# Layer norms applied on ScalarE as scale and bias per token, with the bias formed on GpSimd, in an adaLN transformer block

## The chip, the cores and the metric

The kernel runs on one core of a Trainium2 chip. The metric is the device time of one execution in microseconds, the median of several runs; a separate profiled execution gives the trace. Engines are named as in the profile: PE (TensorE), PEld (its weight loads), ACT (ScalarE), DVE (VectorE), POOL (GpSimd), SP (SyncE, which issues the loads and stores).

## What is computed

One transformer block with adaptive layer norm: 8 blocks (batch rows) of 256 tokens, 128 features. Windowed attention with 16 heads of 8 features, and a mixture of 8 experts of 64 hidden features, of which 2 are chosen.

```python
def _layernorm(x, axis=-1, eps=1e-05):
    m = jnp.mean(x, axis=axis, keepdims=True)
    v = jnp.var(x, axis=axis, keepdims=True)
    return (x - m) / jnp.sqrt(v + eps)
...
    x = L0_attn_x
    mod = (_silu(L0_c) @ L0_wmod).reshape(L0_c.shape[0], 6, 1, -1)
    sa, ca, ga, sb, cb, gb = (mod[:, 0], mod[:, 1], mod[:, 2], mod[:, 3], mod[:, 4], mod[:, 5])
    ga = (2 * (ga >= 0) - 1) * jnp.maximum(jnp.abs(ga), 0.25)
    gb = (2 * (gb >= 0) - 1) * jnp.maximum(jnp.abs(gb), 0.25)
    h = _layernorm(x, axis=-1) * (1 + ca) + sa
    x = x + ga * _L0_attn_ref(h, L0_attn_W_qkv, L0_attn_W_o)
    h = _layernorm(x, axis=-1) * (1 + cb) + sb
    x = x + gb * _L0_ffn_ref(h, L0_ffn_gate_weight, ...)
```

## The kernel before

The 8 blocks go through a software pipeline of 8 steps, written out by hand as one `step` function per engine; semaphores join them. Each engine works strictly in the order of its own `step`. Step i holds the attention of block i, the output projection and second norm of block i-1 (the flag `tail`), the expert layer of block i-2 (`ffn`), and the first norm and the query and key projection of block i+1 (`pre`). In step 1 there is no `ffn`; step 7, the last, has no `pre`; what then remains of blocks 6 and 7 stands behind the loop. The 256 tokens of a block are two tiles (NT = 2) of 128 tokens on the partitions.

A layer norm has four parts. VectorE makes mean and variance (`norm_stats`, L784 and L787, into `mv1` or `mv2`). GpSimd adds eps (L306) and raises to the power -1/2 (L309, `rstd`). VectorE subtracts the mean and multiplies by `rstd`, one instruction per tile (L792, `xn1` for the first norm, `xn2` for the second). TensorE transposes the two tiles (L521), and ScalarE applies the modulation while copying out of PSUM (L389 `h_t`; L411 `h2_t`, then L414 `h2_hi`).

The names that the prediction uses:
- `block_max` (L816) and `row_maximum` (L827, then L834, `shift`) are VectorE's part of the softmax; `subtract_max` (L569) is the TensorE instruction that adds `shift` to the scores; L437 is the exponential on ScalarE.
- The scores are L554, ended by the mask L561. `keep_k` (L807, `k_bd`) and `keep_q` provide keys and queries of the next block; the scores of the next step need both.
- `keep_v` (L404, `v_bd`) is 16 small ScalarE copies. `tanh_gate` (L450), VectorE's `activate` (L907 `gate_a`, L911 `act`), GpSimd's `weigh_experts` (L325, `act_w`), the transposes L638, ScalarE's `act_t` (L454) and the down projection L645 are the expert layer. `low_part` (L337, `h2_lo`) is GpSimd's and follows `act_w` in its queue.
- `logits` (L596) gives the router's input; `route_input` (L419, `ex`) and then `route_compare` (from L872, `exp1`) work on it.
- At the start GpSimd splits the expert weights (L369 `w_hi`, L371 `w_lo`), and VectorE's `finish_modulation` (L959 to L970) makes the gates out of the modulation; it stands behind the first `block_max` of step 0.

In the trace the digits of buffers are left out: `xn`, `h_t`, `x` stand for `xn1` and `xn2`, `h_t` and `h2_t`, `x1`.

## Time and profile before

| | us |
|---|---|
| median of 3 runs | 202.34 (202.28 to 204.95) |
| profiled execution, whole | 204.01 |
| its span, first to last instruction | 202.2 |
| busy: PE / PEld / DVE / ACT / POOL | 157.6 / 131.6 / 151.1 / 99.0 / 49.8 |
| granted TensorE clock, mean | 0.932 |

The span is what the trace's times count in; 1.8 us of the execution lie around it. Busy time is a sum over stages with different limits, so it doesn't say by itself which engine sets the time.

### The profile page before, as it was taken

The page shows a single profiled execution, that of the slowest core. Times are in us where ns is not written, and L with a number is a line of the kernel's source. Part 1 is how long each engine was busy: PE and PEld are TensorE (multiplying, and loading weights), DVE is VectorE, ACT ScalarE, POOL GpSimd, SP SyncE. Part 2 cuts the span into 40 slices and gives each one's busy share as a digit, 9 for nine tenths or more (in the row PEclk, how much of TensorE's full clock was granted, in tenths as well). Part 3 has the DMA queues.
Part 4 walks back from the last instruction along what each step waited for, and adds up shares of the span by engine and source line. Part 5 has one row for each costly group of instructions (what it writes and reads, how often), then busy time and mean ns, then how long its engine had stood idle before and what let it go on. Part 6 is the DMA issues. An engine that isn't in the chain of part 4 may idle for free.

```text
span 202.2 us, 5145 instructions
## 1 busy us (share of the span) xinstructions
PE 157.6 (78%) x1948; PEld 131.6 (65%) x1948; DVE 151.1 (75%) x459; ACT 99.0 (49%) x262; POOL 49.8 (25%) x79
## 2 busy tenths in 40 slices
PE   1766987599877978699777978797779977994954
PEld 1556876488756956588466846595569856873734
DVE  2576346739979897958979897989794987877592
ACT  2162363834394538643567338552943366552311
POOL 5080000320053015302143205320530222225121
PEclk9995899856999999969999999999996999999699
DMA  5800000000000010001000010000000000010001
GB/s 175 268 6 3 0 3 2 28 3 0 3 0 3 0 54 3 3 0 49 6 3 5 22 33 0 0 3 26 5 0 3 26 3 2 0 31 0 0 0 52
DMA packets 5832, 4.17 MB, mean 21 GB/s; under 512 B 816, under 2 KB 5296, under 8 KB 5808
## 3 DMA queue, kind: packets, MB, share of 16 engines
q1 hardware_dynamic: 5664, 3.84, 6.5%
q8 instruction: 15, 0.25, 0.5%
q14 instruction: 9, 0.07, 0.1%
q10 hardware_dynamic: 144, 0.00, 0.0%
HBM read 2.80 MB, written 1.05 MB: 19 GB/s over the span
## 4 chain that ended last, share of the span: by engine, by line
DVE 33%; PE 29%; issue 21%; ACT 13%; POOL 1%; DMA 1%; DVEq 0%; ACTq 0%; POOLq 0%
DVE blkmax L816 9%; ACT v_bd L404 8%; PE ps L569 7%; DVE xn L792 6%; PE ps L645 5%; PE ps L585 4%; DVE gate_a L907 3%; DVE shift L834 3%; PE ps L554 2%; ACT probs L437 2%; DVE eall L862 2%; PE ps L693 2%; DVE row_max L827 1%; PE ps L623 1%; PE ps L521 1%
## 5 line engine op out<-in xcount | busy, mean ns | idle before, releaser
L816 DVE TRANSPOSE_TENSOR_REDUCE blkmax<-ps 128x11 f32<-128x352 f32 x64 | 31.1, 524 | 15.3 <-PE ps L561 15.3
L325 POOL TENSOR_TENSOR act_w<-act,cw 128x512 f32<-128x512 f32 x15 | 15.7, 1045 | 70.1 <-issue 49.5
L585 PE MATMUL ps<-probs,v_bd 128*36 128x64 f32 (+2 forms) x640 | 24.7, 235 | 8.5 <-ACT v_bd L404 8.5
L585 PEld LDWEIGHTS ps<-probs,v_bd 128*36 128x36 f32 x640 | 22.7, 119 | 12.8 <-issue 12.4
L437 ACT ACTIVATE probs<-ps 128x704 f32<-128x704 f32 x32 | 23.0, 755 | 15.0 <-PE ps L569 15.0
L404 ACT ACTIVATE v_bd<-ps 32x64 f32<-32x64 f32 x128 | 27.5, 214 | 1.8 <-PE ps L541 0.4
L569 PE MATMUL ps<-shift,quad_ones 128*128 128x384 f32 x64 | 17.8, 408 | 11.0 <-DVE shift L834 11.0
L554 PEld LDWEIGHTS ps<-q_sb,k_bd 32*128 32x128 f32 x640 | 19.9, 192 | 3.3 <-issue 2.6
L554 PE MATMUL ps<-q_sb,k_bd 32*128 32x96 f32 (+2 forms) x640 | 21.9, 279 | 0.0
L569 PEld LDWEIGHTS ps<-shift,quad_ones 128*128 128x128 f32 x64 | 11.6, 215 | 13.9 <-DVE shift L834 13.3
L450 ACT ACTIVATE tanh_g<-ps 128x512 f32<-128x512 f32 x16 | 9.6, 598 | 19.1 <-PE ps L625 19.0
L645 PE MATMUL ps<-wd_sb,act_t 128*128 128x128 f32 x128 | 17.8, 296 | 0.7 <-ACT act_t L454 0.7
L645 PEld LDWEIGHTS ps<-wd_sb,act_t 128*128 128x128 f32 x128 | 17.2, 214 | 1.0 <-ACT act_t L454 0.9
L807 DVE TENSOR_TENSOR k_bd<-ps,con 128x1024 f32<-128x1024 f32 x8 | 9.8, 1225 | 10.1 <-issue 4.6
L638 PE MATMUL ps<-con,act_w 128*128 128x128 f32 x64 | 10.3, 284 | 7.3 <-POOL act_w L325 5.5
L623 PE MATMUL ps<-w_hi,h_hi 128*128 128x512 f32 x32 | 14.6, 457 | 1.6 <-DVE act L911 1.4
L343 POOL TENSOR_TENSOR out_sb<-y_g,x 128x256 f32<-128x256 f32 x7 | 5.1, 727 | 39.3 <-DVE y_g L939 39.3
L444 ACT ACTIVATE o_t<-ps 36x512 f32<-36x512 f32 x16 | 9.5, 592 | 9.7 <-PE ps L585 9.5
L638 PEld LDWEIGHTS ps<-con,act_w 128*128 128x128 f32 x64 | 6.8, 142 | 10.6 <-POOL act_w L325 7.3
L454 ACT ACTIVATE act_t<-ps 128x512 f32<-128x512 f32 x16 | 9.4, 591 | 8.3 <-PE ps L638 8.3
L625 PE MATMUL ps<-w_hi,h_lo 128*128 128x512 f32 x32 | 13.3, 417 | 0.0
L834 DVE TENSOR_TENSOR shift<-row_max,con 128x256 fp32r<-128x256 f32 x32 | 12.7, 439 | 0.6
(98 smaller groups left out, 287.8 us busy)
## 6 DMA issues: line engine op xcount, KB each, us to landing
x_sb<-x SPq DMA_DIRECT2D x8, 128.0 KB, 2.6
out<-out_sb SPq DMA_DIRECT2D x7, 128.0 KB, 1.8
wgu_sb<-w_gu SPq DMA_DIRECT2D x1, 512.0 KB, 3.9
con<-consts SPq DMA_DIRECT2D x1, 284.0 KB, 3.2
wm_sb<-wmod SPq DMA_DIRECT2D x1, 256.0 KB, 4.0
...
```

The lines of the kernel that those rows point to most:

```text
L325: nc.gpsimd.tensor_tensor(act_w[:, t, :].rearrange("p (e i) -> p e i", e=E), act[:, t, :].rearrange("p (e i) -> p e i", e=E), view(cw[:, t ...
L404: last = nc.scalar.activation(dst, src, ACT.Copy)
L437: nc.scalar.activation(probs[:, t, hgs, cols], ps[:, hgs, cols], ACT.Exp, scale=float(DH) ** -0.5).then_inc(probs_ready, 1)
L554: nc.tensor.matmul(view(ps[:, hg, at:at + 1], [[(QBT - 1) * KB, hi - lo + 1], [1, KB]]), k_bd[rows, kb].rearrange("p g k -> p (g k)"), vie ...
L569: last = nc.tensor.matmul(ps[:, hg, 0:CELLS * KB], quad_ones[:], view(shift[:, hg, 0:1], [[0, 3], [1, QBT * KB]]), start=False, stop=True, ...
L585: last = nc.tensor.matmul(ps[p0:p0 + VW, OB, c0 + lo * KB:c0 + (hi + 1) * KB], v_bd[:, kb, hg, :], view(probs[:, t, hg, at:at + 1], [[-(QB ...
L623: nc.tensor.matmul(ps[:, bank, :], h2_hi[:, tok], w_hi[:, w], start=True, stop=False)
L625: last = nc.tensor.matmul(ps[:, bank, :], h2_lo[:, tok], w_hi[:, w], start=False, stop=True)
L638: last = nc.tensor.transpose(ps[:, W0 + t, c * 128:(c + 1) * 128], act_w[:, t, c * 128:(c + 1) * 128], ident)
L645: last = nc.tensor.matmul(ps[:, down_bank(b, t), t * D:(t + 1) * D], act_t[:, t, c, :], wd_sb[:, c, :], start=(c == 0), stop=(c == NC_ - 1))
L816: nc.vector.tensor_reduce(blkmax[:, t, hg, live(t):live(t) + LIVE], view(ps[:, hg, live(t) * KB:live(t) * KB + 1], [[KB, LIVE], [1, KB]]), ...
L834: nc.vector.tensor_tensor(shift[:, pair * PAIR:(pair + 1) * PAIR].rearrange("p h (q k) -> p (h q) k", k=KB), view(row_max[:, pair * PAIR, ...
```

## The change

The normalised value (x - mean) * rstd is written as x * rstd + (-mean * rstd). GpSimd makes the two numbers per token: a negation of the mean beside the eps addition, and, behind the pow, a product (`shift1`, `shift2`; not the `shift` of the softmax). ScalarE applies them with one Identity activation per tile, with scale and bias read from memory; VectorE's two instructions per norm and the two functions that held them go. VectorE's `norm_stats` gets a wait so that `mv` is not overwritten before GpSimd has used it.

```diff
@@ -300,16 +301,19 @@
 
         @block.gpsimd
         def _(pool):
-            def norm_scale(b, var, mv, veps, step_done, rs, used, ready):
+            def norm_scale(b, var, mv, veps, negm, step_done, rs, rs_done, used, sh, ready):
 
                 wait(pool, var, b, NT, NT)
                 nc.gpsimd.tensor_scalar(veps[:], mv[:, :, 1], EPS, None, ALU.add).then_inc(step_done, 1)
-                wait(pool, step_done, b, 1, 1)
+                nc.gpsimd.tensor_scalar(negm[:], mv[:, :, 0], -1.0, None, ALU.mult).then_inc(step_done, 1)
+                wait(pool, step_done, b, 2, 2)
                 wait(pool, used, b, NT, 0)
-                nc.gpsimd.tensor_tensor(rs[:], veps[:], minus_half[:], ALU.pow).then_inc(ready, 1)
+                nc.gpsimd.tensor_tensor(rs[:], veps[:], minus_half[:], ALU.pow).then_inc(rs_done, 1)
+                wait(pool, rs_done, b, 1, 1)
+                nc.gpsimd.tensor_tensor(sh[:], negm[:], rs[:], ALU.mult).then_inc(ready, 1)
 
             def scale_x(b):
-                norm_scale(b, ln1_var, mv1, veps1, eps1_step, rstd1, xn1_ready, rstd1_ready)
+                norm_scale(b, ln1_var, mv1, veps1, negm1, eps1_step, rstd1, rstd1_step, xn1_ready, shift1, shift1_ready)
 
             def scale_wo(i):
 
@@ -328,7 +332,7 @@
                     view(cw[:, t, :], [[1, E], [0, I]]), ALU.mult).then_inc(actw_ready, 1)
 
             def scale_x1(i):
-                norm_scale(i, ln2_var, mv2, veps2, eps2_step, rstd2, xn2_ready, rstd2_ready)
+                norm_scale(i, ln2_var, mv2, veps2, negm2, eps2_step, rstd2, rstd2_step, xn2_ready, shift2, shift2_ready)
 
             def low_part(i):
 
@@ -382,6 +386,21 @@
 
         @block.scalar
         def _(act_e):
+            def normalise(b, xs, rs, sh, sh_ready, xn, ready):
+
+                wait(act_e, sh_ready, b, 1, 1)
+                for t in range(NT):
+                    nc.scalar.activation(xn[:, t, :], xs[:, t, :], ACT.Identity, scale=rs[:, t:t + 1],
+                                         bias=sh[:, t:t + 1]).then_inc(ready, 1)
+
+            def norm1_apply(b):
+                wait(act_e, xt_ps, b, 1, 0)
+                normalise(b, x_sb[:, b % XBUF], rstd1, shift1, shift1_ready, xn1, xn1_ready)
+
+            def apply_norm2(i):
+                wait(act_e, h2t_ps, i, 1, 0)
+                normalise(i, x1[:, i % 2], rstd2, shift2, shift2_ready, xn2, xn2_ready)
+
             def modulate_x(b):
 
                 wait(act_e, xt_ps, b, 1, 1)
@@ -469,10 +488,14 @@
                     keep_gates(2 * i + 1)
                 if i > 0:
                     keep_v(i)
+                if tail:
+                    apply_norm2(i - 1)
                 if ffn:
                     tanh_gate(i - 2, 1)
                 if tail:
                     modulate_h2(i - 1)
+                if pre and i > 0:
+                    norm1_apply(i + 1)
                 if i < 2:
                     modulate_x(i + 1)
                 if ffn:
@@ -492,11 +515,13 @@
             nc.scalar.preload_act_table(ACT.Exp)
             act_e.wait_ge(c_loaded, 16)
             nc.scalar.activation(ct_t[:], ct_sb[:], ACT.Tanh, scale=0.5).then_inc(tanh_c_ready, 1)
+            norm1_apply(0)
             act_e.wait_ge(mod1_ready, 2)
             modulate_x(0)
             act_e.wait_ge(zeroed, 3)
             keep_q(0)
             keep_v(0)
+            norm1_apply(1)
             steps(step)
 
             keep_o(B - 1)
@@ -504,6 +529,7 @@
             keep_on(B - 1)
             tanh_gate(B - 2, 1)
             keep_act_t(B - 2, 0)
+            apply_norm2(B - 1)
             modulate_h2(B - 1)
             route_input(B - 1)
             keep_act_t(B - 2, 1)
@@ -778,27 +804,18 @@
 
         @block.vector
         def _(dve):
-            def norm_stats(b, xs, stats, stat, mv, var):
+            def norm_stats(b, xs, stats, stat, mv, var, used):
 
                 for t in range(NT):
                     nc.vector.bn_stats(stats[:, t, :], xs[:, t, :]).then_inc(stat, 1)
                 wait(dve, stat, b, NT, NT)
+                wait(dve, used, b, 1, 0)
                 for t in range(NT):
                     nc.vector.bn_aggr(mv[:, t, :], stats[:, t, :]).then_inc(var, 1)
 
-            def normalise(b, xs, mv, rs, rs_ready, xn, ready):
-                wait(dve, rs_ready, b, 1, 1)
-                for t in range(NT):
-                    nc.vector.tensor_scalar(xn[:, t, :], xs[:, t, :], mv[:, t, 0:1], rs[:, t:t + 1],
-                                            ALU.subtract, ALU.mult).then_inc(ready, 1)
-
             def norm1(b):
                 wait(dve, x_loaded[b % XBUF], b // XBUF, 16, 16)
-                norm_stats(b, x_sb[:, b % XBUF], stats1, ln1_stat, mv1, ln1_var)
-
-            def norm1_apply(b):
-                wait(dve, xt_ps, b, 1, 0)
-                normalise(b, x_sb[:, b % XBUF], mv1, rstd1, rstd1_ready, xn1, xn1_ready)
+                norm_stats(b, x_sb[:, b % XBUF], stats1, ln1_stat, mv1, ln1_var, rstd1_step)
 
             def keep_k(b):
 
@@ -930,7 +947,7 @@
 
             def norm2(i):
                 wait(dve, x1_ready, i, 1, 1)
-                norm_stats(i, x1[:, i % 2], stats2, ln2_stat, mv2, ln2_var)
+                norm_stats(i, x1[:, i % 2], stats2, ln2_stat, mv2, ln2_var, rstd2_step)
 
             def gate_output(b):
 
@@ -949,10 +966,6 @@
                 dve.wait_ge(yg_ready, B + t)
                 nc.vector.tensor_tensor(out_last[:, t], y_last[:, t], x1[:, b % 2, t], ALU.add)\
                   .then_inc(last_ready, 1)
-
-            def apply_norm2(i):
-                wait(dve, h2t_ps, i, 1, 0)
-                normalise(i, x1[:, i % 2], mv2, rstd2, rstd2_ready, xn2, xn2_ready)
 
             def finish_modulation():
                 dve.wait_ge(mod_ps, 2)
@@ -986,12 +999,8 @@
                 if pre and i > 0:
                     norm1(i + 1)
                 block_max(i, 1, 0)
-                if tail:
-                    apply_norm2(i - 1)
                 if ffn:
                     activate(i - 2, 1)
-                if pre and i > 0:
-                    norm1_apply(i + 1)
                 block_max(i, 1, 1)
                 row_maximum(i, 1)
                 if tail:
@@ -1011,7 +1020,6 @@
                                            op0=ALU.add, op1=ALU.mult).then_inc(silu_step, 1)
             dve.wait_ge(silu_step, 1)
             nc.vector.tensor_scalar(silu_c[:], silu2_c[:], 0.5, None, ALU.mult).then_inc(silu_step, 1)
-            norm1_apply(0)
             dve.wait_ge(mod_ps, 1)
 
             nc.vector.tensor_copy(mod[:, SA, :], ps[:, W1, SA * B:(SA + 1) * B]).then_inc(mod1_ready, 1)
@@ -1027,7 +1035,6 @@
                                   view(con[:, C_DEN:C_DEN + 1], [[0, NKB * NHG], [1, G]])).then_inc(dens_made, 1)
             keep_k(0)
             norm1(1)
-            norm1_apply(1)
             steps(step)
 
             normalise_o(B - 1)
@@ -1035,7 +1042,6 @@
             residual(B - 1)
             norm2(B - 1)
             activate(B - 2, 1)
-            apply_norm2(B - 1)
             route_compare(B - 1)
             activate(B - 1, 0)
             route_weights(B - 1)
```

The rest of the diff declares the four tiles and the renamed semaphores. No other engine's order is written differently.

ScalarE's queue in step 1 (`keep_v`, then the second norm's `h2_t` and `h2_hi`, then the first norm's `h_t` for block 2), before:

```order
L404 ACTIVATE v_bd<-ps 32x2x4x8 [waits pv_ps,v_ps]
L404 ACTIVATE v_bd<-ps 32x2x4x8 x15
L411 ACTIVATE h2_t<-ps,mod 128x256 [waits h2t_ps]
L414 ACTIVATE h2_hi<-h2_t 128x256 [waits h2_ready]
L389 ACTIVATE h_t<-ps,mod 128x256 [waits v_ps,xt_ps]
L419 ACTIVATE ex<-ps 128x16 [waits logits_ps]
```

And after, the same place:

```order
L423 ACTIVATE v_bd<-ps 32x2x4x8 x15
L393 ACTIVATE xn2<-x1,shift2,rstd2 128x128 [waits shift2_ready]
L393 ACTIVATE xn2<-x1,shift2,rstd2 128x128
L430 ACTIVATE h2_t<-ps,mod 128x256 [waits h2t_ps]
L433 ACTIVATE h2_hi<-h2_t 128x256 [waits h2_ready]
L393 ACTIVATE xn1<-x_sb,shift1,rstd1 128x128 [waits shift1_ready,xt_ps]
L393 ACTIVATE xn1<-x_sb,shift1,rstd1 128x128
L408 ACTIVATE h_t<-ps,mod 128x256 [waits v_ps,xt_ps]
L438 ACTIVATE ex<-ps 128x16 [waits logits_ps]
```

`xn2` now stands between `v_bd` and `h2_t`, and `xn1` of the next block behind `h2_hi`. From step 2 on the tanh of the expert layer follows `xn2`, and the `act_t` copies follow `xn1`:

```order
L393 ACTIVATE xn2<-x1,shift2,rstd2 128x128 [waits shift2_ready,h2t_ps]
L393 ACTIVATE xn2<-x1,shift2,rstd2 128x128
L469 ACTIVATE tanh_g<-ps 128x512 [waits gate_a_ready,up_ps]
L430 ACTIVATE h2_t<-ps,mod 128x256 [waits up_ps,h2t_ps]
L433 ACTIVATE h2_hi<-h2_t 128x256 [waits h2_ready]
L393 ACTIVATE xn1<-x_sb,shift1,rstd1 128x128 [waits shift1_ready,xt_ps]
L393 ACTIVATE xn1<-x_sb,shift1,rstd1 128x128
L473 ACTIVATE act_t<-ps 128x512 [waits actt_ps] x2
L438 ACTIVATE ex<-ps 128x16 [waits route_step,logits_ps]
```

Before, the tanh followed `v_bd` directly, and `act_t` followed `h2_hi`.

VectorE's queue in the same steady step, from the third `block_max` to the `shift` that L569 waits for, before:

```order
L816 TENSOR_REDUCE blkmax<-ps 128x11 [waits rowmax_ready,scores_ps] x2
L792 TENSOR_SCALAR xn2<-x1,mv2,rstd2 128x128 [waits rstd2_ready,h2t_ps]
L792 TENSOR_SCALAR xn2<-x1,mv2,rstd2 128x128
L907 SCALAR_TENSOR_TENSOR gate_a<-tanh_g,ps 128x512 [waits act_ready,tanh_ready]
L911 TENSOR_TENSOR act<-gate_a,ps 128x512 [waits gate_a_ready]
L792 TENSOR_SCALAR xn1<-x_sb,mv1,rstd1 128x128 [waits rstd1_ready,xt_ps]
L792 TENSOR_SCALAR xn1<-x_sb,mv1,rstd1 128x128
L816 TENSOR_REDUCE blkmax<-ps 128x11 [waits rowmax_ready,scores_ps] x2
L827 TENSOR_REDUCE row_max<-blkmax 128x16 [waits shift_ready,blkmax_ready]
L834 TENSOR_TENSOR shift<-row_max,con 128x256 [waits shifted_ps,rowmax_ready]
```

And after:

```order
L833 TENSOR_REDUCE blkmax<-ps 128x11 [waits rowmax_ready,scores_ps] x2
L924 SCALAR_TENSOR_TENSOR gate_a<-tanh_g,ps 128x512 [waits act_ready,tanh_ready]
L928 TENSOR_TENSOR act<-gate_a,ps 128x512 [waits gate_a_ready]
L833 TENSOR_REDUCE blkmax<-ps 128x11 [waits rowmax_ready,scores_ps] x2
L844 TENSOR_REDUCE row_max<-blkmax 128x16 [waits shift_ready,blkmax_ready]
L851 TENSOR_TENSOR shift<-row_max,con 128x256 [waits shifted_ps,rowmax_ready]
```

Four instructions have gone from it; the order of the others is as it was.

## Rows read from the trace of the kernel before

**Rows 1.** The page, part 4: the chain that ended last, shares of the span

```profile
DVE 33%; PE 29%; issue 21%; ACT 13%; POOL 1%; DMA 1%; DVEq 0%; ACTq 0%; POOLq 0%
```

**Rows 2.** The chain in order of time, step 4: start us, us, what

```profile
106.06 1.34 DVE xn L792 x2
```

**Rows 3.** The timeline, step 4: start us, us, engine, line, op, out<-in xcount

```profile
100.48 3.60 ACT L404 ACTIVATE v_bd<-ps 32x64 f32<-32x64 f32 x16
...
102.65 0.71 POOL L309 TENSOR_TENSOR rstd<-veps,minus_half 128x2 f32<-128x2 f32 x1
...
104.11 0.60 ACT L450 ACTIVATE tanh_g<-ps 128x512 f32<-128x512 f32 x1
...
106.28 1.04 POOL L325 TENSOR_TENSOR act_w<-act,cw 128x512 f32<-128x512 f32 x1 [2.91 <-issue]
...
107.28 0.73 POOL L337 TENSOR_TENSOR h_lo<-h_t,h_hi 128x256 fp32r<-128x256 f32 x1
...
107.87 0.51 PE L596 MATMUL ps<-gw_sb,h_t 128*128 128x8 f32 x4
...
109.05 0.97 PE L569 MATMUL ps<-shift,quad_ones 128*128 128x384 f32 x4 [0.67 <-DVE shift L834]
```

**Rows 4.** Groups by line, whole span: xcount, busy us, mean ns, idle before

```profile
L834 DVE TENSOR_TENSOR shift<-row_max,con 128x256 fp32r<-128x256 f32 x32 | 12.7, 439 | 0.6
...
L309 POOL TENSOR_TENSOR rstd<-veps,minus_half 128x2 f32<-128x2 f32 x16 | 11.4, 713 | 1.3
L792 DVE TENSOR_SCALAR xn<-x_sb,mv,rstd 128x128 f32<-128x128 f32 x16 | 11.3, 748 | 2.4 <-POOL rstd L309 2.4
...
L389 ACT ACTIVATE h_t<-ps,mod 128x256 f32<-128x256 f32 x8 | 4.5, 560 | 6.6 <-PE ps L521 6.6
...
L306 POOL TENSOR_SCALAR veps<-mv 128x2 f32<-128x2 f32 x16 | 3.5, 219 | 25.7 <-DVE mv L787 25.4
...
L395 ACT ACTIVATE q_sb<-ps 128x256 f32<-128x256 f32 x8 | 3.1, 385 | 12.0 <-PE ps L534 12.0
```

**Rows 5.** The timeline, start and step 0

```profile
5.09 0.60 DVE L792 TENSOR_SCALAR xn<-x_sb,mv,rstd 128x128 f32<-128x128 f32 x2 [0.96 <-POOL rstd L309]
...
11.66 3.39 DVE L792 TENSOR_SCALAR xn<-x_sb,mv,rstd 128x128 f32<-128x128 f32 x2 [1.22 <-POOL rstd L309]
...
11.92 0.28 PE L561 MATMUL ps<-mask_bf,rep_bf 32*128 32x256 bf16 x4
...
12.62 2.35 POOL L371 TENSOR_TENSOR w_lo<-wgu_sb,w_hi 128x1024 fp32r<-128x1024 f32 x1
...
16.05 0.17 DVE L963 TENSOR_SCALAR mod<-mod 128x8 f32<-128x8 f32 x1
```

**Rows 6.** The timeline, step 1

```profile
42.49 1.12 PE L521 MATMUL ps<-con,xn 128*128 128x128 f32 x4
...
43.82 0.42 ACT L414 ACTIVATE h_hi<-h_t 128x256 fp32r<-128x256 f32 x1
...
43.93 0.99 PE L596 MATMUL ps<-gw_sb,h_t 128*128 128x8 f32 x4 [0.32 <-ACT h_t L411]
...
47.96 1.22 DVE L807 TENSOR_TENSOR k_bd<-ps,con 128x1024 f32<-128x1024 f32 x1
```

**Rows 7.** The timeline, step 7 and behind it

```profile
172.26 1.31 DVE L834 TENSOR_TENSOR shift<-row_max,con 128x256 fp32r<-128x256 f32 x2
...
173.29 0.97 PE L569 MATMUL ps<-shift,quad_ones 128*128 128x384 f32 x4
...
187.68 0.73 POOL L337 TENSOR_TENSOR h_lo<-h_t,h_hi 128x256 fp32r<-128x256 f32 x1 [1.76 <-ACT h_hi L414]
...
188.07 0.37 DVE L872 TENSOR_SCALAR exp<-ex 128x16 f32<-128x16 f32 x1 [2.08 <-ACT ex L419]
```

**Rows 8.** The timeline, behind the loop: the last second norm

```profile
184.66 1.34 DVE L792 TENSOR_SCALAR xn<-x,mv,rstd 128x128 f32<-128x128 f32 x2
```

**Rows 9.** The page, part 2: granted clock in 40 slices of 5.06 us, tenths

```profile
PEclk9995899856999999969999999999996999999699
```

More of the change, by code:

```diff
@@ L144, in program @@
         stats1, mv1 = sb("stats1", [128, NT, 6]), sb("mv1", [128, NT, 2])
-        veps1, rstd1 = sb("veps1", [128, NT]), sb("rstd1", [128, NT])
+        veps1, rstd1, negm1, shift1 = (sb(n, [128, NT]) for n in ("veps1", "rstd1", "negm1", "shift1"))
         xn1 = sb("xn1", [128, NT, D])
@@ L168, in program @@
         stats2, mv2 = sb("stats2", [128, NT, 6]), sb("mv2", [128, NT, 2])
-        veps2, rstd2 = sb("veps2", [128, NT]), sb("rstd2", [128, NT])
+        veps2, rstd2, negm2, shift2 = (sb(n, [128, NT]) for n in ("veps2", "rstd2", "negm2", "shift2"))
         xn2 = sb("xn2", [128, NT, D])
```

5 lines of the change are left out of this document (3 added, 2 removed).

## Prediction

> **What bounds the kernel now.** I read the chain that ended last first, to see which engines can move the end. Its shares [rows 1] are spread: VectorE 33%, TensorE 29%, ScalarE 13%. No engine is the bound throughout; a microsecond taken off VectorE counts only where VectorE is the one that is waited for. So the second view is the chain in order of time, and the third the timeline of one whole step, which shows what stands ready just behind each link.
>
> The steady steps (2 to 6) are 21.1 us long, from one second half's first L569 to the next one's. The normalise lies on the chain there: the second pair of `xn` instructions takes 1.34 us of it [rows 2]. Around it in step 4 [rows 3]: ScalarE copies the values (`v_bd`, 3.60 us from 100.48), and only then makes the tanh (104.11). VectorE forms `gate_a` and `act` from it, GpSimd weighs it (`act_w`, 106.28 to 107.32), TensorE transposes it and makes the logits (107.87 to 108.38). The max subtraction, L569, starts at 109.05. TensorE runs in program order, so L569 needs both VectorE's `shift` and the end of the logits: the logits are done 0.67 us before it starts. That 0.67 us is the number on which the steady steps turn.
>
> **What goes and what comes.** VectorE loses 32 instructions of 128 columns. Those of `x_sb` average 748 ns [rows 4]; a free one takes about 0.34 us, the rest is being held while GpSimd works. Two rows show this: the pair at 11.66 takes 3.39 us and ends about when GpSimd's `w_lo` does, at 14.97 [rows 5], and in step 4 the pair cannot end before `act_w` does.
>
> ScalarE gains 32 instructions, Identity with scale and bias from memory. The same form at 256 columns takes 560 ns [rows 4]. A column costs 0.83 ns, from the tanh over 512 columns at 0.60 us [rows 3] against the copy over 256 at 385 ns [rows 4]; so 128 columns take 560 - 106 = 454 ns and a pair 0.91 us. Bounds: a plain copy's price, 2 x 0.28 = 0.56 us, and the full 256-column price, 1.12 us. I take 0.91, since the row has the same two operands.
>
> The Trainium skill (ScalarE: Activation LUTs, Rules for kernel authors) says that adds and multiplies belong on VectorE, not on ScalarE. By that rule the move loses 0.11 us an instruction against an unheld VectorE one; against the held mean of this trace it wins. The rule speaks against the change, and decides nothing here, since the place in the queue matters more than the price.
>
> GpSimd gains 32 instructions over 2 columns, the negation (219 ns, like `veps` [rows 4]) and the product (0.25 to 0.5 us; the pow takes 713 ns and is the only tiny two-input one shown). With the waits between them a normalisation's numbers come some 0.5 us later. In step 4 the pow of the second norm to be made, the one of the next block, ends at 103.36 [rows 3]; with both norms' additions its numbers are ready at about 104.6 and ScalarE wants them at 107.1; those of the norm in front of it are ready by 103.1 and wanted at 104.1: nothing. GpSimd has nothing queued behind them until `act_w`. VectorE's new wait in `norm_stats` is for a pow one step old: nothing.
>
> **Steady steps, 2 to 6.** The first pair now stands between `v_bd` and the tanh. So tanh, `gate_a`, `act`, `act_w`, the transposes and the logits all come 0.91 us later. VectorE saves the 1.34 us and could have `shift` ready 0.4 us earlier, but TensorE is not free: the logits end at 109.29 in place of 108.38, against 109.05. The step loses 0.91 - 0.67 = 0.24 us. The same point has a second guard: GpSimd's `h2_lo` follows `act_w` (107.28 now, about 108.2 then) and so falls on `shift`, which would be issued at about 108.35. Step 7 shows what happens: `shift` x2 takes 1.31 us [rows 7] where two normally take 0.76 (439 ns each, overlapped a little [rows 4]), and L569 starts 1.03 us after `shift` was issued. This gives nearly the same time. I take +0.25 a step, 5 x 0.25 = +1.25 us; bounds by the pair's price: 0.56 - 0.67 = -0.1 and 1.12 - 0.67 = +0.45.
>
> The second pair stands behind `h2_hi` (free until the `act_t` copies, whose end TensorE's down projection needs only after L569) and moves the copies by 0.9 us to about 109.0 to 109.6: still ahead of the down projection at 110. Hidden; without that cover it would cost its 0.9 us.
>
> **Step 7** has no next block, so there was no 1.34 us pair to save, and logits and L569 followed each other without slack (L569 at 173.29 [rows 7]). The whole 0.91 us shows: +0.95, between 0.6 and 1.1.
>
> **Step 1** is the dearest. TensorE's order is: transposes of `xn2`, transposes of `xn1`, logits, L569. Before, VectorE had made both long ago, and four transposes ran from 42.49 in one go; logits at 43.93 [rows 6]. Now ScalarE makes `xn1` of block 2 only after `h2_t` and `h2_hi`, and `h2_hi` itself needs the first two transposes: it ends at 44.24. The pair ends at 45.2, two transposes at 45.9, and the logits start at about 45.85: +1.9 us on everything behind them. TensorE is at its low clock there (1.2 GHz): the ninth and tenth digits, 40 to 51 us, are 5 and 6 [rows 9]. Where the clock has risen by the time the shifted work runs, some of it goes twice as fast. The least that remains is set by VectorE: `exp1` to `k_bd` (47.96 [rows 6]) is a chain behind the logits that doesn't know TensorE's clock, and the scores of step 2 wait for `k_bd`, which ended 0.7 us before they began. So 1.9 - 0.8 = 1.1 at least, 1.9 at most; I take +1.5.
>
> **The start.** Block 0: `xn1` was made from 5.09 in 0.60 us [rows 5]. Now 0.5 us later and 0.3 us longer, so all work comes about 0.6 us later, up to the first block maximum. That was held until 14.97 behind the pair that waited for `w_lo`, though its scores were complete at 12.2 [rows 5]; it can now start at 12.9. But the next of VectorE's work, `finish_modulation`, has small SBUF-to-SBUF instructions from 16.05 on, and these are held by GpSimd as well: `exp1` of 16 columns took 0.37 us and ended when `h2_lo` did (187.68 + 0.73 [rows 7]). `w_lo` itself starts later, about 13.7, and ends at 16.1. So L963 runs when it ran before: +0.1 us, bounds -2.0 (not held) and +0.7 (the delay in full). The Trainium skill (SBUF — State Buffer, SBUF: two separate sides) states that such VectorE instructions and a GpSimd one exclude each other for the whole instruction. The trace agrees in the rows just named; by the rule alone the start would gain nothing.
>
> **The end.** The last `xn2` took 1.34 us from 184.66, again held by `act_w` [rows 8]. The replacement is 0.5 us of GpSimd and 0.91 us of ScalarE, begun a little earlier since ScalarE needs not wait for `act`: 0.0, between -0.3 and +0.3.
>
> **The sum.** 0.1 + 1.5 + 1.25 + 0.95 + 0.0 = +3.8 us. The profiled execution took 204.01 us (span 202.2 and 1.8 around it), and would take 207.8. The median of the three timed runs is 1.67 us below the profiled one, which is about the price of one of the low-clock stretches below. Set against the median: 202.34 + 3.8 = 206.1 us. All low bounds give -1.3, all high ones +6.0 around it; with the errors independent, 204.7 to 207.5 for this case. A change of 2% is 4.05 us, to 206.4, and that is about what a measurement of this kernel can tell from no change; so this case lies across that line, 0.6 below and 0.4 above.
>
> **Rivals.**
> (a) **Not slower: the hold at the start is what counts.** Place: between 12.9 and 16.05. If the modulation's small instructions get through before or beside `w_lo`, the gates, and all behind them, come 2.0 us earlier. For it: no instruction of fewer than 16 columns is shown held. Against it: the hold of `exp1`. It decides if the rest of the sum is under 2.0, which needs the ScalarE pair near 0.7 us (steady 0, step 7 +0.7) and step 1 near 1.1: 202.34 - 2.0 + 1.8 = 202.1 us. With the pair at 0.91 it gives 204.1.
> (b) **Slower by over 2%: the clock.** Steps 3 and 6 of the profile each show a fall of the granted clock behind L569 (the slices at 86 and 152 us stand at 6, their neighbours at 9 [rows 9]); those steps measure 22.7 to 22.9 us by the same L569, 1.6 more than steps 2, 4 and 5 with the same work. Ahead of each fall TensorE had the gaps around `act_w` and L569. The change makes these gaps longer in every step, 0.25 us, and inserts one of 2 us in step 1. One more such stretch gives 206.1 + 1.6 = 207.7, two 209.3. Against it: with the same gaps two steps of five fell and three did not, so it hangs on more than their length.
> (c) **The move is free:** another wait has the slack, and only step 1 and noise remain, or the gain of VectorE shows in full (0.91 - 1.34 a step, -2.1 in all, which cancels steps 1 and 7 in good part): 202.3 to 203.5. For it: the 1.34 us lies on the chain. Against: TensorE's order and 0.67 us of slack.
>
> **How the numbers follow.** The forecast has 0.50, (a) 0.14, (b) 0.27, (c) 0.09. Slower by over 2%: 0.50 x 0.4 + 0.27 = 0.47. Faster by over 2% (under 198.3) only if (a) and (c) come together: 0.02. Within 2%: 0.51. The range has the forecast's case whole, most of (b), and (a) and (c) from 202.9 up: 202.9 to 209.2.
>
> **What would show it.** In the new profile: `xn` of 128 columns on ScalarE at about 454 ns; L569 of the steady steps right behind the logits, with `shift` ready or held by `h2_lo`; in step 1 a TensorE wait of about 2 us before the second pair of transposes, released by ScalarE's `xn`; L963 starting when `w_lo` ends; VectorE's busy time down by some 14 to 16 us, most of it now idle. The forecast is wrong if the pair costs well under 0.67 us, if L963 runs before 15 us, or if more steps show the granted clock at 0.50.

## The result and the profile after

The changed kernel takes 208.97 us (207.25 to 210.31, 4 runs) against 202.31 us (200.98 to 204.95, 4 runs) for the kernel before on the same chip: ratio 1.0347, 95% interval 1.0239 to 1.0456, 6.7 us slower. Two more measurements of it gave 1.0275 and 1.0325 (below). The forecast was 206.1 us. The profiled execution took 208.63 us, 4.62 more than the one before; the forecast for it was 3.8 more. The ratios leave disturbed runs out, so they differ a little from the quotient of the medians.

The page of the changed kernel, parts 1, 2 and 4:

```profile
PE 159.1 (77%) x1948; PEld 133.1 (64%) x1948; DVE 139.3 (67%) x427; ACT 113.2 (55%) x294; POOL 56.7 (27%) x111
...
PEclk9999999958997999999996999999988999999697
...
PE 29%; issue 25%; DVE 22%; ACT 16%; POOL 5%; DMA 1%; DVEq 0%; POOLq 0%; ACTq 0%
```

VectorE's share of the chain fell from 33% [rows 1] to 22%, and its busy time by 11.8 us. Nothing was gained: what VectorE no longer does was put into another queue on the same chain. The groups by line, over the whole span:

```profile
L851 DVE TENSOR_TENSOR shift<-row_max,con 128x256 fp32r<-128x256 f32 x32 | 15.5, 524 | 0.6
...
L393 ACT ACTIVATE xn<-x,shift,rstd 128x128 f32<-128x128 f32 x16 | 7.0, 486 | 1.3 <-POOL shift L313 1.2
L393 ACT ACTIVATE xn<-x_sb,shift,rstd 128x128 f32<-128x128 f32 x16 | 6.9, 479 | 2.8 <-POOL shift L313 2.8
...
L313 POOL TENSOR_TENSOR shift<-negm,rstd 128x2 f32<-128x2 f32 x16 | 3.2, 203 | 1.2
```

ScalarE's price is close to the forecast's 454 ns: 479 and 486 ns one by one, 0.86 and 0.88 us for a pair, since the two overlap a little (0.91 was forecast). GpSimd's product takes 203 ns. The softmax `shift` went from 439 ns [rows 4] to 524 ns.

The timeline of step 4 (start us, us, engine, line, op, out<-in, xcount) shows where the pair stands:

```profile
102.87 0.91 ACT L423 ACTIVATE v_bd<-ps 32x64 f32<-32x64 f32 x4
...
103.80 0.88 ACT L393 ACTIVATE xn<-x,shift,rstd 128x128 f32<-128x128 f32 x2
...
104.15 0.20 POOL L313 TENSOR_TENSOR shift<-negm,rstd 128x2 f32<-128x2 f32 x1
104.70 0.60 ACT L469 ACTIVATE tanh_g<-ps 128x512 f32<-128x512 f32 x1
...
105.33 0.69 DVE L924 SCALAR_TENSOR_TENSOR gate_a<-tanh_g,ps 128x512 f32<-128x512 f32 x1 [1.40 <-ACT tanh_g L469]
...
106.87 1.04 POOL L329 TENSOR_TENSOR act_w<-act,cw 128x512 f32<-128x512 f32 x1 [2.53 <-issue]
106.89 0.63 PE L664 MATMUL ps<-con,act_w 128*128 128x128 f32 x4 [1.16 <-DVE act L928]
...
107.87 0.73 POOL L341 TENSOR_TENSOR h_lo<-h_t,h_hi 128x256 fp32r<-128x256 f32 x1
107.91 1.31 DVE L851 TENSOR_TENSOR shift<-row_max,con 128x256 fp32r<-128x256 f32 x2
107.97 0.66 PE L664 MATMUL ps<-con,act_w 128*128 128x128 f32 x4 [0.46 <-POOL act_w L329]
...
108.47 0.51 PE L622 MATMUL ps<-gw_sb,h_t 128*128 128x8 f32 x4
...
108.94 1.47 PE L595 MATMUL ps<-shift,quad_ones 128*128 128x384 f32 x4
...
110.62 2.89 PE L671 MATMUL ps<-wd_sb,act_t 128*128 128x128 f32 x16
```

`v_bd` ends at 103.78 and the tanh starts 0.92 us later; in [rows 3] it followed at once (104.08, 104.11). The logits (L622) now end as L595, the max subtraction (L569 before), begins: the 0.67 us of slack is used up. `shift` is held by `h_lo`, 1.31 us for the pair. So both guards fell as forecast, and from the end of `v_bd` to L595 (L569 before) it is now 5.16 us, before 4.97. Of TensorE's two waits for `act` and `act_w` the first was shorter in the kernel before, 0.26 us where the rows above have 1.16:

```profile
106.29 0.63 PE L638 MATMUL ps<-con,act_w 128*128 128x128 f32 x4 [0.26 <-DVE act L911]
...
107.38 0.66 PE L638 MATMUL ps<-con,act_w 128*128 128x128 f32 x4 [0.46 <-POOL act_w L325]
...
110.07 1.95 PE L645 MATMUL ps<-wd_sb,act_t 128*128 128x128 f32 x16
```

What the forecast did not have is in the rows of L595 and L671 of the changed kernel. L595 takes 1.47 us where it took 0.97 [rows 3], and the down projection 2.89 us against the 1.95 of L645. The same timeline cut into two windows (us, busy time of PE, PEld, DVE, ACT, POOL, granted clock, DMA share, GB/s):

```profile
98.20:108.90 10.70, 7.83 (x112) 6.35 (x112) 7.72 (x21) 8.78 (x27) 5.46 (x11) 1.00 0.00 1
108.90:112.90 4.00, 4.00 (x19) 3.85 (x19) 2.62 (x13) 2.41 (x5) 0.00 (x0) 0.57 0.01 4
```

The granted clock fell from 2.4 to 1.2 GHz 0.2 us after L595 began, and stayed there for 3.4 us. From the starts of the max subtraction, two to a step, the two executions compare like this. "First half" goes from the first L569 or L595 of a step to its second, "second half" from there to the next step. "The rest" begins with the second half of step 7.

| | before | after | difference | forecast |
|---|---|---|---|---|
| start, to the first L569/L595 of step 1 | 33.80 | 33.33 | -0.47 | +0.1 |
| step 1, to that of step 2 | 20.85 | 20.66 | -0.19 | +1.5 |
| steps 2 to 6 | 108.83 | 111.40 | +2.57 | +1.25 |
| - of it, a first half | 10.52 | 10.71 | +0.19 | +0.25 |
| - of it, second halves at 12.1 to 12.2 us and not 10.6 | 2 of 5 | 3 of 5 | +1.6 | 0 |
| step 7, first half | 9.81 | 10.71 | +0.90 | +0.95 |
| the rest | 28.91 | 30.70 | +1.79 | 0.0 |

The rest has one more stretch at the low clock, over the last down projection (L671, 3.30 us; L645 took 2.01 before):

```profile
200.92 3.30 PE L671 MATMUL ps<-wd_sb,act_t 128*128 128x128 f32 x16
```

Start and step 1 came out better in this pair of executions only because of the clock. In step 1 the kernel before ran 10.2 us at 1.2 GHz, from 38.8 us on [rows 9], the changed one 6.8 us. At the start the row of the granted clock misleads: it shows full speed for the changed kernel up to 40 us, but the same eight matmuls that ran at full speed in the kernel before are slow in it (before, then after):

```profile
12.13 1.06 PE L682 MATMUL ps<-silu_c,wm_sb 128*128 128x8 f32 x8
...
13.59 1.88 PE L708 MATMUL ps<-silu_c,wm_sb 128*128 128x8 f32 x8
```

One matmul of L719 (L693 before) takes 421 ns until 20.3 us and 275 ns from 20.4 us on in the changed kernel; before, it takes about as much, 408 to 421 ns, up to the last one at 21.5 us, and the granted clock rose at 21.8 us. So TensorE came to 2.4 GHz 1.3 us earlier in the changed kernel's execution. The row shows full speed until the first change that the trace has recorded, here the one at 20.4 us. So this one pair of profiles can't settle the sum, and the experiments had to separate order from clock.

### The profile page after: what moved, and what is told of

The parts are those of the page before. It is cut to its first block, busy times and chain, and to the rows that moved or that the text cites. A ratio compares the mean times of both kernels' runs of the same rounds, so it can differ in the third digit from the quotient of the medians.

```text
span 206.8 us, 5191 instructions
## 1 busy us (share of the span) xinstructions
PE 159.1 (77%) x1948; PEld 133.1 (64%) x1948; DVE 139.3 (67%) x427; ACT 113.2 (55%) x294; POOL 56.7 (27%) x111
## 4 chain that ended last, share of the span: by engine, by line
PE 29%; issue 25%; DVE 22%; ACT 16%; POOL 5%; DMA 1%; DVEq 0%; POOLq 0%; ACTq 0%
ACT v_bd L423 9%; PE ps L595 7%; DVE blkmax L833 6%; PE ps L671 5%; POOL act_w L329 4%; PE ps L580 3%; ACT xn L393 3%; ACT probs L456 3%; PE ps L664 2%; DVE eall L879 2%; PE ps L611 2%; PE ps L547 2%; DVE shift L851 2%; PE ps L622 1%; PE ps L719 1%
## 5 line engine op out<-in xcount | busy, mean ns | idle before, releaser
L611 PE MATMUL ps<-probs,v_bd 128*36 128x64 f32 (+2 forms) x640 | 23.1, 227 | 8.4 <-ACT v_bd L423 8.4
L456 ACT ACTIVATE probs<-ps 128x704 f32<-128x704 f32 x32 | 23.0, 755 | 11.8 <-PE ps L595 11.8
L611 PEld LDWEIGHTS ps<-probs,v_bd 128*36 128x36 f32 x640 | 21.1, 114 | 12.7 <-issue 12.3
L595 PE MATMUL ps<-shift,quad_ones 128*128 128x384 f32 x64 | 18.4, 417 | 7.7 <-DVE shift L851 7.7
L580 PEld LDWEIGHTS ps<-q_sb,k_bd 32*128 32x128 f32 x640 | 20.3, 195 | 3.3 <-issue 2.4
L671 PE MATMUL ps<-wd_sb,act_t 128*128 128x128 f32 x128 | 20.0, 321 | 0.7 <-ACT act_t L473 0.7
L671 PEld LDWEIGHTS ps<-wd_sb,act_t 128*128 128x128 f32 x128 | 19.4, 237 | 1.0 <-ACT act_t L473 0.9
L595 PEld LDWEIGHTS ps<-shift,quad_ones 128*128 128x128 f32 x64 | 12.0, 221 | 10.3 <-DVE shift L851 9.5
L824 DVE TENSOR_TENSOR k_bd<-ps,con 128x1024 f32<-128x1024 f32 x8 | 9.8, 1225 | 11.8 <-issue 6.2
L924 DVE SCALAR_TENSOR_TENSOR gate_a<-tanh_g,ps 128x512 f32<-128x512 f32 x16 | 10.9, 682 | 9.7 <-ACT tanh_g L469 8.4
L851 DVE TENSOR_TENSOR shift<-row_max,con 128x256 fp32r<-128x256 f32 x32 | 15.5, 524 | 0.6
```

Source lines behind the costliest of these rows:

```text
L456: nc.scalar.activation(probs[:, t, hgs, cols], ps[:, hgs, cols], ACT.Exp, scale=float(DH) ** -0.5).then_inc(probs_ready, 1)
L580: nc.tensor.matmul(view(ps[:, hg, at:at + 1], [[(QBT - 1) * KB, hi - lo + 1], [1, KB]]), k_bd[rows, kb].rearrange("p g k -> p (g k)"), vie ...
L595: last = nc.tensor.matmul(ps[:, hg, 0:CELLS * KB], quad_ones[:], view(shift[:, hg, 0:1], [[0, 3], [1, QBT * KB]]), start=False, stop=True, ...
L611: last = nc.tensor.matmul(ps[p0:p0 + VW, OB, c0 + lo * KB:c0 + (hi + 1) * KB], v_bd[:, kb, hg, :], view(probs[:, t, hg, at:at + 1], [[-(QB ...
L671: last = nc.tensor.matmul(ps[:, down_bank(b, t), t * D:(t + 1) * D], act_t[:, t, c, :], wd_sb[:, c, :], start=(c == 0), stop=(c == NC_ - 1))
L851: nc.vector.tensor_tensor(shift[:, pair * PAIR:(pair + 1) * PAIR].rearrange("p h (q k) -> p (h q) k", k=KB), view(row_max[:, pair * PAIR, ...
```

## The experiments

All are edits of the changed kernel unless said otherwise. "Falls" are second halves of steps 2 to 6 that take 11.8 us or more in the one profiled execution, with a stretch at the low clock over them; without one they take 10.6 to 10.7 us.

| run | median us | ratio to before, 95% | first half | falls |
|---|---|---|---|---|
| e1_norm1 | 199.19 | 0.982 (0.974 to 0.991) | 9.81 | 0 |
| e3_step1 | 206.82 | 1.016 (1.006 to 1.027) | 10.71 | 2 |
| e4_tanhfirst | 200.66 | 0.979 (0.968 to 0.991) | 9.80 | 0 |
| e5_both | 197.96 | 0.976 (0.968 to 0.985) | 9.82 | 0 |
| r1_after | 209.20 | 1.028 (1.018 to 1.037) | 10.71 | 3 |
| e2_norm2 | 212.96 | 1.054 (1.045 to 1.064) | 11.42 | 3, one of 6.8 us |
| e6_split | 205.97 | 1.024 (1.018 to 1.031) | 10.71 | 2 |
| e7_both_split | 195.50 | 0.970 (0.962 to 0.977) | 9.80 | 0 |
| e8_after_fill | 203.76 | 1.012 (1.008 to 1.017) | 10.71 | 0 |
| e9_norm2_fill | 204.11 | 1.011 (1.004 to 1.017) | 11.42 | 0 |
| e10_before_fill | 200.60 | 0.997 (0.991 to 1.003) | 10.52 | 0 |
| r2_after | 209.29 | 1.033 (1.024 to 1.041) | 10.71 | 2 |

The first four shared one chip and its runs of the kernel before (203.36 us), the next four another (202.21), the last four a third (202.16). Only the ratios compare across the three. For e1, e3, e4, e5, r1 and e6 the interval lies on one side of 1 but has 2% inside it: the sign is clear, a change of over 2% is not. The profiled executions of r1_after (209.24 us), e3_step1 (209.13) and e2_norm2 (214.94) were among the longer ones of their kernels, so their falls may be more than usual.

**One norm alone.** e1_norm1 gives norm 2 back to VectorE, e2_norm2 gives norm 1 back; the functions that return are those of the kernel before.

```diff
# e1_norm1: second norm as before
-                if tail:
-                    apply_norm2(i - 1)
# e2_norm2: first norm as before
-                if pre and i > 0:
-                    norm1_apply(i + 1)
```

> Only the first norm is applied on ScalarE; the second norm is applied by VectorE as before. Theory 1 (the loss comes from the place of the xn2 pair ahead of the tanh): the tanh of the steady steps is back at the end of the value copies, so the steady half step from L569 to L569 falls below the 10.53 us of the kernel before, to about 9.9 to 10.0, step 7 costs nothing, and start and step 1 still cost 0.3 and 1.5 us: 201 to 202.5 us, ratio to before 0.99 to 1.00. Theory 2 (the added ScalarE work, or longer gaps that lower the clock, cost by themselves wherever they stand): half of the loss stays, 205 to 206 us.

> Only the second norm is applied on ScalarE; VectorE keeps the first. Theory 1 (order): the tanh comes 0.9 us later, and VectorE still has the 1.34 us xn1 pair between act and the last block maximum, so nothing is saved there: the half step rises from 10.52 to about 11.4 us, 5 x 0.9 + 0.9 in step 7 = 5.4 us above before without the clock, more than the whole change, though only half the work is moved; 208 to 210 us. Rival (each ScalarE instruction has its price): half of the whole change, about 205 us.

The two halves of the change have opposite signs. Norm 1 alone is 1.8% faster than the kernel before: its pair stands behind `h2_hi`, where ScalarE has time, and leaves VectorE. Norm 2 alone is 5.4% slower, worse than the whole change: it puts its pair ahead of the tanh and keeps the 1.34 us pair of norm 1 on VectorE as well. Each expectation had the sign and erred in size: e1 came in some 2 us faster than expected, e2 3 us slower. The profile of e2_norm2 has a first half of 11.42 us, 0.9 over that of before, and three falls of five, one of them twice as long (second halves of 12.31, 12.20 and 13.40 us; the expectation of e9_norm2_fill below says four). In all that is 13.7 us at the low clock in steps 2 to 6, where the kernel before has 6.8. TensorE there in step 4:

```profile
109.42 0.44 PE L551 MATMUL ps<-con,xn 128*128 128x128 f32 x2
111.03 0.63 PE L668 MATMUL ps<-con,act_w 128*128 128x128 f32 x4 [1.16 <-DVE act L943]
112.11 0.66 PE L668 MATMUL ps<-con,act_w 128*128 128x128 f32 x4 [0.46 <-POOL act_w L337]
...
113.78 0.97 PE L599 MATMUL ps<-shift,quad_ones 128*128 128x384 f32 x4 [0.67 <-DVE shift L866]
```

From the `act_w` transposes to the max subtraction it waits three times, 1.16 + 0.46 + 0.67 = 2.29 us. The changed kernel has the first two (1.62 us), the kernel before 0.26, 0.46 and 0.67 (1.39 us). The queues explain 0.9 us a step for e2, 4.5 us in steps 2 to 6 and 0.9 in step 7; it lost 10.8, which made me doubt the equal clock of my sum.

**The place in ScalarE's queue.** e4_tanhfirst lets the tanh go first:

```diff
-                if tail:
-                    apply_norm2(i - 1)
                 if ffn:
                     tanh_gate(i - 2, 1)
+                if tail:
+                    apply_norm2(i - 1)
```

> The whole change, but in the steady steps and step 7 ScalarE makes the second half's tanh ahead of the xn2 pair. Theory 1: the tanh is 0.9 us earlier, the half step falls from 10.71 to about 10.0 us (then ex, or shift held by h2_lo, sets it), step 7 gains 0.9 us: 3.5 to 4.5 us less than the whole change, ratio to before 1.00 to 1.015. Theory 2 (clock, engine price): within 1 us of the whole change.

Two calls exchanged, and 2.8 to 3.5% slower became 2.1% faster. The timeline of step 4:

```profile
99.89 0.60 ACT L469 ACTIVATE tanh_g<-ps 128x512 f32<-128x512 f32 x1
...
100.39 0.87 ACT L393 ACTIVATE xn<-x,shift,rstd 128x128 f32<-128x128 f32 x2
...
102.06 1.04 POOL L329 TENSOR_TENSOR act_w<-act,cw 128x512 f32<-128x512 f32 x1 [1.63 <-issue]
102.08 0.63 PE L664 MATMUL ps<-con,act_w 128*128 128x128 f32 x4 [0.26 <-DVE act L928]
...
103.65 0.51 PE L622 MATMUL ps<-gw_sb,h_t 128*128 128x8 f32 x4
...
104.12 0.97 PE L595 MATMUL ps<-shift,quad_ones 128*128 128x384 f32 x4
```

From the tanh to L595 it is the same 4.2 us as in the changed kernel (104.70 to 108.94); the whole stretch has moved up by the 0.91 us. TensorE's first wait is 0.26 us again, nothing waits for `shift`, and there is no fall in the steady steps. The expected gain was about half of the measured one: the order is worth 0.91 us in each of six first halves, and the falls that went with it came on top.

**Step 1.** e3_step1 makes `xn1` of block 2 ahead of `h2_t`; e5_both does that and the tanh first.

```diff
+                if i == 1:
+                    norm1_apply(2)
                 if tail:
                     modulate_h2(i - 1)
-                if pre and i > 0:
+                if pre and i > 1:
                     norm1_apply(i + 1)
```

> The whole change, but in step 1 alone ScalarE makes xn1 of block 2 ahead of h2_t and h2_hi, so that TensorE's four transposes run in one go again. Theory 1 (order in the queue): 1.1 to 1.9 us less than the whole change, ratio to before about 1.025, and no TensorE wait for ScalarE's xn in step 1. Rival (the clock pays it back, since the shifted work runs at the high clock): under 0.5 us less.

> Both moves in ScalarE's queue together: xn1 ahead of h2_t in step 1, the tanh ahead of the xn2 pair in the steps with an expert layer. Theory 1: the two gains add, 5 to 6 us less than the whole change, ratio to before 0.99 to 1.005, so the move of the norms itself costs nothing and VectorE's time comes off. Theory 2: still 2% or more above before.

In the changed kernel TensorE waits in step 1 as forecast:

```profile
40.87 0.68 PE L547 MATMUL ps<-con,xn 128*128 128x128 f32 x2
...
42.18 0.42 ACT L433 ACTIVATE h_hi<-h_t 128x256 fp32r<-128x256 f32 x1
42.51 0.86 ACT L393 ACTIVATE xn<-x_sb,shift,rstd 128x128 f32<-128x128 f32 x2
...
43.42 0.69 PE L547 MATMUL ps<-con,xn 128*128 128x128 f32 x2 [1.87 <-ACT xn L393]
```

With e3_step1 the four transposes run in one go again:

```profile
42.96 1.12 PE L549 MATMUL ps<-con,xn 128*128 128x128 f32 x4
...
44.39 0.99 PE L624 MATMUL ps<-gw_sb,h_t 128*128 128x8 f32 x4 [0.32 <-ACT h_t L430]
```

In executions with the same 10.2 us at the low clock in step 1, that step takes 20.85 us before, 20.99 (e3_step1) and 21.00 (e5_both) with the early pair, and 21.84 (e1_norm1) with the late one: the wait costs 0.85 to 1.0 us there. In the runs e3_step1 lies 1.1 to 1.8% under the three measurements of the whole change, with intervals that overlap: the profiles show the step, the runs don't contradict it. e5_both came out at 0.976, better than the 0.99 to 1.005 expected, and can't be told from e4_tanhfirst (0.979).

**The start.** e6_split moves GpSimd's split of the weights (`w_hi`, `w_lo`) from the start to step 1; e7_both_split is e5_both with that.

```diff
-            nc.gpsimd.tensor_copy(w_hi[:], wgu_sb[:]).then_inc(w_parts, 1)
-            pool.wait_ge(w_parts, 1)
-            nc.gpsimd.tensor_tensor(w_lo[:], wgu_sb[:], w_hi[:].bitcast(F32), ALU.subtract)...
+                if i == 1:  # behind scale_wo(0), the same three lines
```

> The whole change, with GpSimd's split of the expert weights (w_hi, w_lo) moved from the start to step 1, behind the first scaled output weight, so that it can't hold VectorE's small instructions in step 0. If those are held by w_lo (my term for the start), L976 runs at its input, 0.7 to 2 us earlier, and the time falls by 0.7 to 2 us against the whole change. If they are not held, nothing changes.

> The two moves in ScalarE's queue (xn1 ahead of h2_t in step 1, tanh ahead of the xn2 pair) and the weight split moved to step 1, together. The gains add: 0.7 to 2 us under the version with the two moves alone, 195.5 to 197.5 us, ratio to before 0.96 to 0.975. If the start is not on the path, as with the two moves alone, 0.975 to 0.98.

The changed kernel beside `w_lo`:

```profile
14.13 2.35 POOL L375 TENSOR_TENSOR w_lo<-wgu_sb,w_hi 128x1024 fp32r<-128x1024 f32 x1
...
15.73 0.77 DVE L976 TENSOR_SCALAR mod<-mod 128x8 f32<-128x8 f32 x1
```

e6_split, where GpSimd does nothing there:

```profile
15.45 0.19 DVE L973 COPY mod<-ps 128x32 f32<-128x32 f32 x1 [0.84 <-PE ps L709]
15.68 0.17 DVE L977 TENSOR_SCALAR mod<-mod 128x8 f32<-128x8 f32 x1
```

The same instruction of 8 columns takes 0.77 us and ends as `w_lo` does (16.50 and 16.48), or 0.17 us. In e8_after_fill, where `w_lo` (13.99 to 16.33 us) met another one, that one was held:

```profile
14.12 2.24 DVE L988 TENSOR_SCALAR gsize<-gabs 128x16 f32<-128x16 f32 x1
```

So the hold is shown, and it is worth 0.65 us at the first L595 (18.21 against 18.86 us), not the 2.0 us of rival (a): without it the step waits for the copy of the modulation's matmuls, which comes 0.06 us earlier only. By the first L595 of step 1 little of it is left: 33.29 in e6 and 33.07 in e7, against 33.33 to 33.42 in the three executions of the changed kernel. In the runs e6 can't be told from r1_after (1.024 and 1.028): the medians differ by 3.2 us, the ratios by 0.6 us only. e7_both_split is the fastest kernel of all, 3.0% under the kernel before, as expected.

**Is it the clock?** r1_after and r2_after are the changed kernel unchanged. In e8, e9 and e10 TensorE repeats transposes that it makes anyway, into the same place, where it would stand idle: 10 more in each of steps 2 to 7, and no wait, order or other engine is touched. e8 is made from the changed kernel, e9 from e2_norm2, e10 from the kernel before.

```diff
-            def transpose_norm(b, bank, xn, ready, done):
+            def transpose_norm(b, bank, xn, ready, done, again=0):
                 wait(pe, ready, b, NT, NT)
+                for _ in range(again):
+                    for t in range(NT):
+                        nc.tensor.transpose(ps[:, bank, t * 128:(t + 1) * 128], xn[:, t, :], ident)
...
+                if t == 0 and b < B - 2:
+                    for c in range(NC_):
+                        nc.tensor.transpose(ps[:, W0, c * 128:(c + 1) * 128],
+                                            act_w[:, 0, c * 128:(c + 1) * 128], ident)
...
-                transpose_norm(i, W2, xn2, xn2_ready, h2t_ps)
+                transpose_norm(i, W2, xn2, xn2_ready, h2t_ps, 3 if 1 <= i < B - 1 else 0)
```

> The whole change once more, unaltered, with more rounds, to part structure from clock. Over its runs the span should rise by 0.2 us for each us at the low clock, as in the four first runs; the line should stand 3 to 4 us above that of the kernel before at equal low-clock time (my forecast's terms without the clock: +3.8). The rest of a ratio of about 1.03 is then time at the low clock, some 10 us more of it per run. If instead the lines lie 6 us apart, my terms are too small by themselves.

> The whole change, and TensorE transposes what it transposes anyway once more into the same place, where it would otherwise idle: the pair of xn2 transposes three times more (6 transposes, about 0.95 us by the 0.157 us of one in the group of four that takes 0.63 us) ahead of the gap of 1.16 us, and the first four transposes of act_w once more (0.63 us) ahead of the gap of 0.46 us, in steps 2 to 7. No wait is removed; outputs are the same. Theory A (the clock falls behind L595 because TensorE stood idle too much ahead of it): the steady steps show no granted clock of 0.5, low time per run drops from 28 to some 18 us or less, and in spite of up to 0.17 us a step (1.0 us in all) that the added work pushes the logits, the kernel takes 205 to 207 against 209 for the whole change: ratio 1.012 to 1.025. Theory B (the falls hang on something else, such as the place in the run or the length of a step): the same number of falls, 209 to 210.5. If it costs more than 1 us a step, my count of the cover is wrong.

> Only the second norm on ScalarE, as in the run that measured 1.054 with falls of the clock in four steady steps of five, and the same filler on TensorE as in the run above (10 more transposes in each of steps 2 to 7). There the logits stand 0.67 us ahead of L599 in the trace, so the filler should cost nothing. Theory A: the falls of the steady steps go, the half steps of 12.2 to 13.4 us fall to 10.6, and the time drops by 4 to 7 us: 206 to 209. Theory B: 212 to 214 as without the filler.

> The kernel before with the same filler. Its profiled execution had falls in two steady steps of five, 1.6 us each, and the logits have 0.67 us of slack, so that the filler should be hidden. Theory A: no falls in the steady steps, 198.5 to 201, ratio 0.98 to 0.993. Theory B: 202 to 203.

> The whole change, unchanged, beside its filled form on the same chip: 207 to 210, ratio 1.025 to 1.035, low time per run 24 to 31 us, falls in two or three steady steps.

Theory A held, and for e8 and e9 by more than I had expected. e8 does more work than r2_after and takes less time: 4.1 us less by the ratios (1.012 and 1.033, intervals apart), 5.5 us by the medians (203.76 and 209.29). TensorE of e8 in step 4:

```profile
103.09 0.87 PE L548 MATMUL ps<-con,xn 128*128 128x128 f32 x6
103.80 0.38 PE L550 MATMUL ps<-con,xn 128*128 128x128 f32 x2
...
104.69 0.63 PE L668 MATMUL ps<-con,act_w 128*128 128x128 f32 x4 [0.50 <-DVE act L935]
105.15 1.28 PE L671 MATMUL ps<-con,act_w 128*128 128x128 f32 x8
...
106.26 0.51 PE L625 MATMUL ps<-gw_sb,h_t 128*128 128x8 f32 x4
106.74 0.96 PE L598 MATMUL ps<-shift,quad_ones 128*128 128x384 f32 x4
...
107.76 1.95 PE L678 MATMUL ps<-wd_sb,act_t 128*128 128x128 f32 x16
```

The wait ahead of the `act_w` transposes is 0.50 us where it was 1.16, the next one is gone, and the half step is the same 10.71 us: the filler cost nothing. What changed is behind it, L598 at 0.96 and the down projection at 1.95 us. The page's rows of the granted clock, e8 and then r2_after:

```profile
PEclk9995899999999999999999999999999999995888
```

```profile
PEclk9999999988999999889999999699999999699678
```

All second halves of steps 2 to 6 are at 10.6 to 10.7 us in e8, e9 and e10, against 2 or 3 of five at 11.9 to 13.4 in the same kernels without it. The dearest case gains most: norm 2 alone goes from 1.054 to 1.011. The kernel before gains 0.3%, less than theory A gave it and not to be told from nothing by its interval; of the three it was the one with the least time at the low clock in these steps. What its profile gains there (108.83 to 105.57 us) it loses in part behind step 7, where e10 has 10.2 us at the low clock and the kernel before 3.4.

r1_after was also to compare the two orders at an equal clock. A line through 15 runs of the changed kernel and 44 of the kernel before, with the time at the low clock taken from each run's mean granted clock, has the changed kernel 3.7 us above at equal low time and 0.25 us more for each microsecond of it. That is rough (the runs of the kernel before scatter by 1.4 us around it, and the low clock of the first 20 us isn't always counted), but it is what the filler gives as well.

So e8 and e10 are the pair that the forecast's sum was made for: the two orders, with the steady steps at the high clock in both. Their profiled spans are 201.9 and 198.1 us, and both have 10.2 us at the low clock in the part behind step 7:

| part | e10_before_fill | e8_after_fill | difference | forecast |
|---|---|---|---|---|
| start | 33.20 | 33.48 | +0.28 | +0.1 |
| step 1 | 18.68 | 19.96 | +1.28 | +1.5 |
| steps 2 to 6 | 105.57 | 106.50 | +0.93 | +1.25 |
| step 7, first half | 9.69 | 10.71 | +1.02 | +0.95 |
| the rest | 30.96 | 31.25 | +0.29 | 0.0 |
| span | 198.1 | 201.9 | +3.8 | +3.8 |

The start is the one row with unequal clocks: by the matmuls' durations TensorE came to 2.4 GHz at 20.4 us in e10 and at 21.3 us in e8. The profiled executions of the changed kernel in which it did so at 20.4 and 20.7 us (the first one and r2_after) have 33.33 and 33.42, +0.13 and +0.22. By the medians the pair differs by 3.2 us (203.76 - 200.60), by the ratios by 3.1 (0.0153 x 202.2).

## Why the prediction was right and wrong

**Right: the mechanism, and all terms of the sum that concern order.** ScalarE's pair stands ahead of the tanh and costs 0.88 us (0.91 forecast), of which 0.67 is slack: +0.19 a step against +0.25, shown by the rows of step 4 and by e4_tanhfirst, where it goes with the order. Step 7 has no slack and paid +0.90 to +1.02 (0.95). Step 1 paid +1.28 at the high clock and 0.85 to 1.0 at the low one (1.5): TensorE's wait was 1.87 us (1.9 forecast), and a little more of it was made good behind it than I took. The start was held by `w_lo`, as forecast (+0.1, measured +0.13 with the clock rising at the same time): the argument came from one 16-column row [rows 7], and e6_split showed it with 0.77 and 0.17 us. The Trainium skill (SBUF — State Buffer, SBUF: two separate sides) states that exclusion for the whole instruction, and the trace agrees with these two figures. With TensorE's gaps filled in both kernels the total is 3.8 us in the profiles and 3.1 to 3.2 in the runs, against +3.8. That the profiles give the very number is luck: step 1 and the steady steps came out 0.5 us under the forecast, and start, step 7 and the rest 0.5 us over it. The second pair behind `h2_hi` was hidden, as said: the `act_t` copies (107.55 and 108.67) ended at 109.27, before the down projection at 110.62.

**Wrong: the equal clock of the sum.** The step that failed is "Set against the median: 202.34 + 3.8 = 206.1 us". It carries the kernel before's low-clock stretches over unchanged: the sum has no term for the clock. I had it only as rival (b), with 0.27. It came, on top of the order. By the ratios of the third chip, the whole change costs 6.6 us; 3.1 of it is order (e8 against e10), and 3.5 is what the filler gives back more in the changed kernel (4.1 us) than in the kernel before (0.6 us). By the medians these are 7.1, 3.2 and 3.9 (5.5 and 1.6). The result lies in the range of 202.9 to 209.2 only because the range took in most of rival (b); the forecast's own case ended at 207.5. The prediction had the place, the gaps around `act_w` and L569, and their growth: 1.39 to 1.62 us a half step, +0.23 against "0.25 us". It had the price as well: 207.7 with one more such stretch, 209.3 with two. That the result fits two is partly luck, since in the profiled pair the steady steps and the part behind step 7 have one more stretch each, while start and step 1 ran faster than before. What it lacked was the reason to make this the main case. It gave the clock 0.27 because two steps of five fell with equal gaps. The profiles have, by the waits from the `act_w` transposes to the max subtraction: no falls with 0.72 us (e1, e4, e5, e7) and none with 0.50 to 1.18 us (the filled kernels), two with 1.39 (one profile), two or three with 1.62 (five profiles), three with 2.29, one of them twice as long (one profile). So the ends differ clearly; whether 0.23 us more a step adds a fall is not shown by these counts, and rests on what the filler gives back. The clock also cost more in the part behind step 7, where the three profiles have one to two stretches of 3.4 us more than before.

**Rival (a)** fell with the row of L976 at 0.77 us. **Rival (c)** fell with the first half at 10.71. The rule that the prediction weighed (the Trainium skill, ScalarE: Activation LUTs, Rules for kernel authors: adds and multiplies on VectorE) is not borne out here as a rule: with the same operation on ScalarE, at 479 to 486 ns against 748 held ones [rows 4], e1_norm1 and e4_tanhfirst are 1.8 and 2.1% faster than before, e2_norm2 5.4% slower. Smaller misses: VectorE's busy time fell by 11.8 us, not by 14 to 16, since `shift` is held longer (12.7 to 15.5 us in all); GpSimd's product took 0.20 us, under the 0.25 to 0.5 allowed; and the low bounds of the terms add up to about -1.1 and the high ones to +6.25, not to -1.3 and +6.0, on which nothing else rests.

**What stays open.** Equal gaps still gave a fall in some steps and none in others (two or three of five in three profiles of the changed kernel); the filler shows that the falls go when TensorE waits less, not what decides each one. The stretches behind step 7 have no filler ahead of them, and in e8 and e10 they last 10.2 us where the kernel before had 3.4. The filler on top of e5_both or e7_both_split was not tried; neither has falls in its steady steps.
